# Attention block with a gated output: a new plan of the steps, and places of the values' products and of the output's turning taken from a table per group of heads

## The reference, cut to what matters

```python
x = L0_attn_x                                   # 4 batches x 512 positions x 256 channels, float32
xn = layernorm(x)
q, k, v = split(xn @ Wqkv.T + bqkv)             # 16 heads of 16 channels each
q, k = rope(q), rope(k)                         # rotary positions
att = softmax(where(causal, q @ k.T / sqrt(16), -inf))
s = (att @ v) @ Wo.T + bo
g = silu(einsum('btd,rde->bte', xn, factors) / sqrt(8) + bias)
out = x + s * g
```

## Time and profile before

| what | number |
|---|---|
| median of 3 runs | 225.77 us (225.0 to 225.97) |
| the profiled execution | 225.08 us |
| its span, first to last instruction | 223.3 us |
| PE busy | 210.4 us, 94% of the span |
| DVE busy | 167.8 us, 75% |
| ACT busy | 137.9 us, 62% |
| POOL busy | 112.8 us, 51% |

### The profile page before, as it was taken

One profiled execution on the slowest core, in us unless ns is written; L12 is line 12 of the kernel. 1 busy time (PEld: TensorE's weight loads), 2 busy tenths in 40 slices (PEclk: granted clock), 3 DMA queues, 4 the chain that ended last, 5 costly groups with the idle time before them and its releaser, 6 DMA issues.

```text
span 223.3 us, 5566 instructions
## 1 busy us (share of the span) xinstructions
PE 210.4 (94%) x2193; PEld 141.0 (63%) x2193; DVE 167.8 (75%) x268; ACT 137.9 (62%) x268; POOL 112.8 (51%) x104
## 2 busy tenths in 40 slices
PE   6999998998999999999999999999999999999892
PEld 2478866666657556667775575658756665585471
DVE  7779949979999797786976699669947796741233
ACT  2333461359664875893558978891278658869930
POOL 7884999753930860400779200954750034029912
PEclk9999999999999999999999999999999999999999
DMA  5996915101520340150036300035155000002002
GB/s 147 365 358 205 218 53 193 44 3 42 176 71 9 130 155 6 58 203 27 4 101 207 126 3 6 0 117 181 43 188 191 3 6 3 3 9 94 3 0 97
DMA packets 15790, 21.47 MB, mean 96 GB/s; under 512 B 2068, under 2 KB 9236, under 8 KB 15764
## 3 DMA queue, kind: packets, MB, share of 16 engines
q1 hardware_dynamic: 15248, 20.06, 27.5%
q0 software_dynamic: 192, 0.52, 1.0%
q10 hardware_dynamic: 324, 0.52, 0.8%
HBM read 6.16 MB, written 2.10 MB: 37 GB/s over the span
## 4 chain that ended last, share of the span: by engine, by line
PE 66%; DVE 18%; POOL 7%; ACT 4%; issue 4%; DVEq 0%; POOLq 0%
PE ring_ps L484 16%; DVE rowmax L832 10%; PE ring_ps L550 9%; PE ring_ps L521 9%; PE ring_ps L607 6%; PE ring_ps L626 5%; PE ring_ps L494 5%; PE ring_ps L502 5%; PE ring_ps L676 3%; PE ring_ps L642 2%; ACT probs L944 2%; PE ring_ps L681 2%; DVE parts L805 2%; PE ring_ps L583 1%; DVE by_sin L807 1%
## 5 line engine op out<-in xcount | busy, mean ns | idle before, releaser
L832 DVE TENSOR_REDUCE rowmax<-ring_ps 128x2 f32<-128x768 f32 (+3 forms) x103 | 89.5, 915 | 22.6 <-PE ring_ps L502 22.2
L944 ACT ACTIVATE probs<-ring_ps 128x512 f32<-128x512 f32 x160 | 83.5, 608 | 23.3 <-PE ring_ps L502 16.6
L484 PE MATMUL ring_ps<-probs,vaug 128*17 128x256 f32 (+3 forms) x528 | 37.8, 426 | 1.0 <-ACT probs L944 0.7
L521 PE MATMUL ring_ps<-stack_k,stack_q 62*128 62x512 f32 (+3 forms) x256 | 37.2, 355 | 1.6 <-DVE rowmax L832 0.6
L550 PE MATMUL ring_ps<-stack_q,stack_k 64*128 64x128 f32 (+3 forms) x256 | 36.4, 351 | 0.5
L502 PE MATMUL ring_ps<-ident_bf,masks 64*128 64x128 bf16 (+1 forms) x640 | 36.0, 210 | 0.0
L521 PEld LDWEIGHTS ring_ps<-stack_k,stack_q 62*128 62x128 f32 x256 | 20.9, 185 | 11.1 <-issue 7.8
L714 POOL TENSOR_TENSOR parts<-parts 128x1024 fp32r<-128x1024 f32 x7 | 16.7, 2381 | 21.9 <-ACT parts L915 21.9
L484 PEld LDWEIGHTS ring_ps<-probs,vaug 128*17 128x17 f32 x528 | 13.8, 97 | 22.0 <-issue 16.5
L550 PEld LDWEIGHTS ring_ps<-stack_q,stack_k 64*128 64x128 f32 x256 | 21.1, 185 | 8.9 <-issue 6.3
L626 PE MATMUL ring_ps<-wvg_sb,xnT 128*128 128x512 f32 x96 | 25.1, 405 | 1.2 <-DVE rowmax L832 0.8
(11 more groups left out here) (95 smaller groups left out, 279.3 us busy)
## 6 DMA issues: line engine op xcount, KB each, us to landing
stack_q<-parts SPq DMA_DIRECT2D x48, 128.0 KB, 2.6
stack_k<-parts SPq DMA_DIRECT2D x42, 128.0 KB, 2.6
probs<-factors SPq DMA_DIRECT2D x2, 1024.0 KB, 8.4
...
stack_k<-parts POOLq DMA_DIRECT2D x4, 128.0 KB, 3.6
```

Source lines behind the costliest of these rows:

```text
L484: mm = pe.matmul(ps[32 * s:32 * s + HD + 1, first:end], vaug[:, b % 2, j, h, :], probs[:, slot, col + first - j * P:col + end - j * P], st ...
L521: pe.matmul(ps[:, col:col + (tile + 1) * P], qk[b % 2][0][rows, h // SIDES, tile * P:(tile + 1) * P], qk[b % 2][1][rows, h // SIDES, 0:(ti ...
L832: taking = dve.tensor_reduce(of_both, keys, AX_X, ALU.max)
L944: act.activation(probs[:, chunk % PROB_SLOTS, :], ps[:, :], ACT.Exp, scale=float(HD) ** -0.5).then_inc(taken[kind], 1)
```

## The change

VALUES_AT becomes a table with a pair of numbers for each of the first 15 groups of heads: the place (in chunks, 0 to 10) of values and take_o, and that of turn_o, between the next group's scores. `attention_steps` and `spread` read it. All other tables of the plan (CHAINS, ATTENTION, MAXIMA, END, JOINED) get new numbers. No instruction is added or taken out; 41 joined pairs become 38. The order of the steps changes on every engine, in most places by one or two steps.

```diff
@@ attention_steps
-    s = []
+    s = [(c // 2 * 2, ("scores", b, g * EXP_CHUNKS + c)) for c in range(EXP_CHUNKS)]
     before = b * GROUPS + g - 1
-    gb, gg = before // GROUPS, before % GROUPS
-    for c in range(EXP_CHUNKS):
-        s.append((c, ("scores", b, g * EXP_CHUNKS + c)))
-        if before >= 0:
-            s += [(c, (kind, gb, gg)) for kind, at in VALUES_AT if at == c]
-    return s
+    if before >= 0:
+        values_at, turned_at = VALUES_AT[before]
+        which = divmod(before, GROUPS)
+        s += [(values_at, ("values",) + which), (values_at, ("take_o",) + which), (turned_at, ("turn_o",) + which)]
+    return sorted(s, key=lambda entry: entry[0])
@@ spread
-    return [(start + (end - start) * (c // 2 * 2) / EXP_CHUNKS, step) for c, step in steps]
+    return [(start + (end - start) * at / EXP_CHUNKS, step) for at, step in steps]
@@ tables
-VALUES_AT = (("values", 3), ("take_o", 3), ("turn_o", 7))
+VALUES_AT = ((1.8, 9.5), (2.4, 7.9), (2.4, 4.3), (3.8, 6.5), (2.8, 6.9), (2.9, 8.9), (0.5, 5.9), (2.9, 7.1),
+             (2.1, 7.4), (3.9, 9.5), (0.5, 8.7), (3.9, 6.5), (3.3, 9.5), (4.8, 8.7), (5.6, 9.5))
...
```

More of the change, by code:

```diff
@@ L157 @@
 CHAINS = (
[L158 to L169, removed]
-     ("load", 3, 3.163), ("store", 0, 4.465), ("store", 1, 7.296)),
@@ L187 @@
-    (("stats", 0, 3.671), ("normalise", 0, 3.797), ("turn_x", 0, 4.076), ("turn_x", 1, 4.102),
-     ("project_qk", 0, 4.266), ("rstd", 0, 4.378), ("project_qk", 1, 4.496), ("rotate", 0, 4.646),
-     ("high", 0, 4.917), ("low", 0, 4.981), ("project_qk", 2, 5.208), ("project_qk", 3, 5.231), ("rotate", 1, 5.335),
-     ("stack", 0, 5.638), ("stack", 1, 5.850), ("high", 1, 5.894), ("project_vg", 0, 6.142),
-     ("project_vg", 1, 6.310), ("low", 1, 6.370), ("project_vg", 2, 6.657), ("shift", 0, 6.824),
-     ("project_vg", 3, 6.888), ("bias_vg", 0, 7.172), ("gate_tanh", 0, 7.342), ("shift", 1, 7.358),
-     ("turn_y", 0, 7.840), ("gate", 0, 10.780), ("stack", 2, 11.869), ("stack", 3, 14.996)))
@@ new lines @@
+    (("stats", 0, -1.656), ("rstd", 0, 0.387), ("normalise", 0, 1.575), ("turn_x", 0, 1.760), ("turn_x", 1, 1.772),
+     ("project_qk", 0, 1.950), ("project_qk", 1, 2.003), ("rotate", 0, 2.087), ("project_qk", 2, 2.267),
+     ("high", 0, 2.327), ("project_qk", 3, 2.362), ("low", 0, 2.372), ("stack", 0, 2.484), ("stack", 1, 2.578),
+     ("rotate", 1, 3.015), ("project_vg", 0, 3.046), ("high", 1, 3.118), ("project_vg", 1, 3.325),
+     ("project_vg", 2, 3.331), ("stack", 2, 3.428), ("project_vg", 3, 3.444), ("low", 1, 3.793), ("shift", 0, 4.288),
+     ("bias_vg", 0, 4.295), ("gate_tanh", 0, 4.537), ("stack", 3, 4.660), ("shift", 1, 5.490), ("turn_y", 0, 7.113),
+     ("gate", 0, 7.201), ("turn_y", 1, 7.291), ("project_o", 0, 7.520), ("project_o", 1, 7.693),
+     ("store", 0, 18.653), ("store", 1, 22.335)),
@@ new lines @@
+    (("stats", 0, 3.530), ("normalise", 0, 3.794), ("turn_x", 0, 4.100), ("turn_x", 1, 4.116), ("rstd", 0, 4.183),
+     ("project_qk", 0, 4.319), ("project_qk", 1, 4.542), ("rotate", 0, 4.587), ("high", 0, 4.939), ("low", 0, 5.001),
+     ("project_qk", 2, 5.328), ("stack", 0, 5.389), ("project_qk", 3, 5.399), ("rotate", 1, 5.671),
+     ("stack", 1, 5.718), ("high", 1, 6.098), ("low", 1, 6.262), ("project_vg", 0, 6.353), ("project_vg", 1, 6.451),
+     ("project_vg", 2, 6.628), ("shift", 0, 6.861), ("project_vg", 3, 6.939), ("bias_vg", 0, 7.040),
+     ("gate_tanh", 0, 7.385), ("shift", 1, 7.392), ("turn_y", 0, 7.930), ("gate", 0, 9.857), ("stack", 2, 12.460),
+     ("stack", 3, 13.003)))
```

71 lines of the change are left out of this document (37 added, 34 removed).

## The result

The changed kernel takes 222.88 us (median of six runs, 221.68 to 223.64) against 225.6 us, a ratio of 0.9873 with an interval of 0.9845 to 0.9901. The profiled execution took 223.5 us, with a span of 221.5.

What follows compares the result with a forecast made beforehand. It took DVE's maxima from 40 to 60 us, then PE, as the bound. Start +1.8 and give-back -1.9 made -0.1 on 225.08, 225.7 on the median; it said 225.6 us, range 224.0 to 227.5.

Steps and rivals of the forecast that it cites:

- Part 2: Start, ACT: the keys' last transfers issue behind normalise.1.0, at 28.0 to 28.5; first maxima at 31.3, +1.4 us (1.0 to 2.0).
- Part 3: At shift.0.0, near 49 us: DVE waits longer for ACT's half of the maxima, +0.4 us (0 to 0.6).
- the first two terms of Part 4: PE's idle time at 118 to 128 us and 140 to 145 us shrinks as steps move: -0.5 and -0.2 us.
- Part 4: PE's idle time behind 100 us, 2.59 us, partly comes back as steps are rearranged: -1.9 us (-0.5 to -2.6).
- What bounds the kernel: DVE from 40 to 60 us, so late first maxima delay everything; later PE, with 2.59 us idle behind 100 us.
- Part 1: Start: memsets moved behind DVE's first tiles, both then about 400 ns; PE ready at 29.4, -0.5 us (-0.7 to 0).
- the terms behind 164 us: PE's waits at turn_o, 176 to 192 us, and at turn_y.3.0 and end_values in the tail: -0.8 and -0.6 us.
- the +0.2 for the pairs across the ring's end: On DVE: nine pairs of maxima instead of six lie across the ring's end, +0.2 us (0 to +0.5).
- the faster one: Start: late transfers don't hold PE, needing issue before some 26.5 or a give-back at its bounds; 223.8 us, chance 0.25.
- The slower clock: PE behind its new wait of about 2 us at the start: lower rate, +1.7 at most, 226.6 us; chance 0.03.

Runs made afterwards that it cites:

- the run with one step of the tail put back: The changed kernel with turn_y.3.0 ahead of values.3.2 on PE again, nothing else moved; its profile has keep_warm at 8.55 us; 222.99 us, ratio 0.9900.
- the mended late part: The kernel before, with PE's order exactly that of the changed kernel behind values.2.1 (164 us) and its own up to there; ratio 0.9946.
- the run with the early warm-up: The changed kernel with turn_y.3.0 ahead of values.3.2 on PE again, keep_warm at 8.55 us in its profile; 222.99 us, ratio 0.9900.
- the middle alone: The kernel before with the changed plan from the first maxima (30 us) to values.2.1 (164 us); 1.0080, or 0.9934 with rotate.3.1 ahead of project_o.1.1's gate product.
- the run with the places alone: The kernel before with the new table of places for values, take_o and turn_o, all due times as before; ratio 1.0269.

## Why the prediction was wrong, point by point

The forecast was 2.7 us too high. About half of that, 1.4, is Part 2, the step that failed. The other half is the middle: it gave 1.5 us, where Part 3 and the first two terms of Part 4 come to +0.4 - 0.5 - 0.2 = -0.3. The late part came out much as said.

**What bounds the kernel** was read rightly. PE's idle time behind 100 us was 2.59 us, and most of it went. That a delay of the first maxima moves everything behind it is borne out by the short warm-up in the kernel before: its first maxima are 1.5 us later, and its span is 1.4 longer. What the prediction left out is that the changed start takes a wait away behind the first maxima as well, so that a delay there is not the start's whole price.

**Part 1** had the mechanism right, 410 ns for both tiles, and the size too where the warm-up ends early: PE was ready for the first maxima at 29.43 in the run with one step of the tail put back, where the prediction had 29.4. With a warm-up as late as in the changed kernel's own profile nothing of it is left: PE was ready there at 31.10 - 0.44 = 30.66, and in the mended late part, which has the start of the kernel before and keep_warm at 9.81, the first maxima start at 30.64.

**Part 2** is the step that failed. It laid the issue of the transfers behind the 2.08 us of normalise, at 28.0 to 28.5. ACT issues them when rstd.1.0 is done. The run with the early warm-up shows this step by itself, since all that leads up to it came as forecast: normalise.1.0 starts at 26.25 (25.9 to 26.4 in the prediction), PE is ready at 29.43. But the issue comes at 26.31, PE waits 0.51 us and not 2, and the first maxima start at 29.94 and not at 31.3: +0.04 in place of +1.4. The landing of 2.6 was right (2.7). The step alone, in the kernel before, measured +0.36 (1.0002 to 1.0030), and -0.3 when undone in the changed kernel. That the changed kernel's first maxima start at 31.10, near the forecast, is luck: its warm-up was late. Behind the first maxima the start gives some 0.6 us back, by high.0.1's new place on ACT among other things, which the order ahead of the prediction shows and the prediction didn't price.

**Part 3**: DVE's wait at shift.0.0 grew from 1.56 us to 1.75, so +0.2 for +0.4. But the stretch round it gained about 1.0 us. Only a part of that is located. In the profile of the middle alone DVE's products of project_qk.1.0 and 1.1 stand back to back ahead of first_shift, and DVE is through all three by 41.03 us; with first_shift between them it is through by 41.40 in the kernel before, at first maxima at the same time (29.87 and 29.90). That is 0.37. The rest up to 76 us isn't traced to single steps and stays open.

**Part 4**: the terms behind 164 us, -0.8 and -0.6, came as 1.54 in the trace and 1.2 in the time. The terms between 118 and 145 us, -0.5 and -0.2, mostly didn't: between values.1.1 and values.2.0 the traces of the two kernels differ by 0.3 us. For the tail the sum was right and the reason half wrong, as the run with turn_y.3.0 put back showed. No run tests the +0.2 for the pairs across the ring's end, nor the three joins by themselves.

**The rivals**: the faster one, 223.8, was right in kind: the late transfers hold PE by 0.44 us in the changed kernel's profile, by 0.51 with the early warm-up, and by 0.76 at most in the other profiles that have them. Its condition, an issue before some 26.5, came true with the early warm-up (26.31), but not for its reason: rstd.1.0 ended not earlier but later than in the kernel before (26.25 against 25.58). The slower clock didn't occur in the changed kernel while PE had work, but it is real: behind waits of 1.93 and 2.04 us of PE two traces show 0.50, and by the traces it cost 1.6 and 1.4 us, inside the 0 to 1.7 of the fourth rival. By the Trainium skill, "TensorE: Matmul & The Clock Gate", section What's actually happening, idle time brings the clock down to 1.2 GHz; the level in these two traces agrees. Such a wait doesn't always do it: behind the 1.95 us of the run with the places alone the clock stayed at 1.00.
